# A selective-scan layer on one core: softplus in one function, three of sixteen products on GpSimd, the residual added by TensorE, row stores issued by SP

## The reference, cut to what matters

```
xi, z = split(xs @ W_in)                    # 64 channels each
xc = silu(causal_conv4(xi) + conv_b)
dt_r, B, C = split(xc @ W_x)                # 2, 16, 16
dt = softplus(dt_r @ W_dt + b_dt)           # 64 channels
h  = exp(dt * A) * h + dt * x * B           # per step, 64 channels x 16 states
y  = sum over states of h * C
out = x + ((y + xc * D_skip) * silu(z)) @ W_out
```

## Time and profile before

| | |
|---|---|
| median of three runs | 3129.49 us (3125.74 to 3132.32) |
| profiled execution, first to last instruction | 3123.6 us |
| around the span (median less span) | 5.9 us |
| triangle layers, first scan of the scan layer | to about 1254 us, at 1295.6 us |
| one chunk of the scan layer, steady | 56.7 us |
| busy: PE, DVE, ACT, POOL | 82%, 80%, 61%, 66% |

### The profile page before, as it was taken

The page is one execution under the profiler, slowest core; times in us unless marked ns, Lnnn a source line. Parts: engine busy times, 40 slices in busy tenths (PEclk is TensorE's granted clock), DMA queues, the critical chain, the costliest instruction groups (busy, mean ns, idle before and its releaser), DMA issues.

```text
span 3123.6 us, 40760 instructions
## 1 busy us (share of the span) xinstructions
PE 2573.1 (82%) x12954; PEld 756.1 (24%) x12954; DVE 2485.6 (80%) x2176; ACT 1914.4 (61%) x2402; POOL 2065.3 (66%) x1284
## 2 busy tenths in 40 slices
PE   5888878888788775688888888888888888888886
PEld 1233123331233211222222222222222222222221
DVE  5655656555555544599999999999999999999998
ACT  4534654346543343667777777677777776777772
POOL 2543245432444313298898888988988889889886
PEclk9999999999999988799999999999999999999999
DMA  4797327863279647667677677676775766767765
GB/s 162 241 325 212 102 67 255 294 205 102 72 241 313 192 133 181 132 146 181 147 165 167 144 177 163 148 181 148 162 170 145 179 160 148 180 148 162 171 145 117
DMA packets 257701, 537.53 MB, mean 172 GB/s; under 512 B 39608, under 2 KB 150656, under 8 KB 256688
## 3 DMA queue, kind: packets, MB, share of 16 engines
q1 hardware_dynamic: 215328, 444.01, 53.7%
q0 software_dynamic: 19040, 64.24, 7.7%
q10 hardware_dynamic: 23216, 27.74, 3.7%
HBM read 396.55 MB, written 139.33 MB: 172 GB/s over the span
## 4 chain that ended last, share of the span: by engine, by line
POOL 29%; issue 27%; PE 5%; DVE 2%; DMA 2%; ACT 1%; SPq 1%; POOLq 0%; ACTq 0%; DVEq 0%
POOL m_hs L500 18%; POOL m_sp_v L517 2%; POOL m_dtx L527 2%; POOL m_gated L506 2%; DMA t_tile<-band_out 1%; POOL m_dt L524 1%; POOL m_dt L520 1%; SPq L913 1%; DVE m_pb L472 1%; PE t_bank L1096 1%; PE t_bank L1057 1%; PE t_bank L1021 1%; POOL t_xc L1481 1%; DVE m_hs L477 1%; PE m_misc L230 0%
## 5 line engine op out<-in xcount | busy, mean ns | idle before, releaser
L500 POOL TENSOR_TENSOR m_hs<-m_hs,m_cs 128x1024 f32<-128x1024 f32 x512 | 1203.6, 2358 | 288.4 <-DVE m_hs L477 288.4
L477 DVE TENSOR_TENSOR_SCAN m_hs<-m_da,m_pb 128x1024 f32<-128x1024 f32 x512 | 1170.7, 2287 | 29.3 <-ACT m_da L399 4.2
L399 ACT ACTIVATE m_da<-m_dtb,m_a_neg 128x1020 f32<-128x1020 f32 x512 | 576.6, 1144 | 275.9 <-DMA m_dtb<-dt_rows 254.1
L282 PE MATMUL m_pb<-m_dtx,late 64*128 64x512 f32 x2048 | 583.5, 646 | 150.2 <-DVE m_hs L477 146.9
L265 PE MATMUL m_py<-m_hs,late 128*64 128x512 f32 x2048 | 565.8, 631 | 104.8 <-POOL m_hs L500 104.0
L472 DVE TENSOR_TENSOR m_pb<-m_pb,m_bs 128x1024 f32<-128x1024 f32 x512 | 619.7, 1210 | 20.9 <-PE m_pb L282 20.9
L1481 POOL TENSOR_TENSOR t_xc<-t_xc,big 128x512 f32<-128x512 f32 x96 | 120.1, 1271 | 338.8 <-DVE big L1387 338.8
L282 PEld LDWEIGHTS m_pb<-m_dtx,late 64*128 64x128 f32 x2048 | 163.4, 188 | 567.3 <-DVE m_hs L477 457.5
L1021 PE MATMUL t_bank<-late,t_lwin 128*128 128x256 f32 x816 | 217.3, 404 | 63.3 <-ACT big L1260 34.0
L1359 DVE SCALAR_TENSOR_TENSOR t_xc<-t_bank,t_vec,t_xc 128x512 f32<-128x512 f32 x96 | 72.0, 750 | 244.2 <-PE t_bank L1057 244.2
L1248 ACT ACTIVATE t_sq<-t_bank 128x512 f32<-128x512 f32 x192 | 105.5, 598 | 245.3 <-PE t_bank L1096 245.2
(11 more groups left out here) (166 smaller groups left out, 3591.3 us busy)
## 6 DMA issues: line engine op xcount, KB each, us to landing
m_dtb<-dt_rows SPq DMA_DIRECT2D x512, 512.0 KB, 6.1
late<-right_factor POOLq DMA_DIRECT2D x102, 512.0 KB, 5.5
right_factor<-t_tile SPq DMA_DIRECT2D x192, 256.0 KB, 3.5
t_tile<-band_out SPq DMA_DIRECT2D x183, 256.0 KB, 4.2
band_out<-t_vwin SPq DMA_DIRECT2D x48, 512.0 KB
band_out<-t_vwin SPq DMA_DIRECT2D x48, 480.0 KB
dt_rows<-m_dt ACTq DMA_DIRECT2D x64, 256.0 KB, 3.2
t_xc<-in_x_cm SPq DMA_DIRECT2D x4, 2048.0 KB, 14.6
```

Source lines behind the costliest of these rows:

```text
L282: m = nc.tensor.matmul(pb[s % 2][:, half(n)], spread[rows, dg, :], dtx[par][rows, half(q)], start=True, stop=True)
L399: nc.scalar.activation(da[:, s % DA_RING, :, 1:T], dtb[s % DTB_RING][:, :].rearrange("p (r t) -> p r t", t=T)[:, :, 1:T], ACT.Exp, scale=a ...
L477: nc.vector.tensor_tensor_scan(hs[:, s % H_RING, :], da[:, s % DA_RING, :, :].rearrange("p r t -> p (r t)"), pb[s % 2][:, :], 0.0, ALU.mul ...
L500: nc.gpsimd.tensor_tensor(hs[:, s % H_RING, :], hs[:, s % H_RING, :], cs[q][:, :], ALU.mult).then_inc(hc_ready, 1)
```

## The change

- dt: ScalarE applies Softplus straight from PSUM (two half tiles, table set "softplus" loaded before, the exp set after). The seven activations and GpSimd's six half tiles go; so do the buffers `sp_*`.
- Steps 5, 10 and 15 (`POOL_U`): TensorE writes the spread dt*x to `misc` instead of `pb`, ScalarE copies it to an SBUF tile `ub` (ring of two), GpSimd multiplies it by B there, and VectorE runs only the scan, with both inputs in SBUF.
- The residual: TensorE multiplies `xm` (moving operand, step 1 KB) by the identity `eye` into `py[1]`, on top of which the output product adds; ScalarE copies the sum to `fin`. VectorE's L484 goes.
- `dt_rows` and the stores of the result are issued by SP, shares 13 and 14, instead of ScalarE at share 14.
- `x` and `z` of the next chunk stand together in TensorE's share 5 and are taken together by one `silu`; the order of the uses of `misc` changes.
- The loop over chunks is written out in full.

```diff
+    POOL_U = (5, 10, 15)
+    UB_RING = 2
+        ub = [sb(f"ub{i}", [P, W]) for i in range(UB_RING)]
...
+        FIRST_USE = {op: i for i, op in enumerate(("x", "z", "dt", "bq0", "cq0"))}
+        USE = {op: i for i, op in enumerate(("u5", "bq1", "cq1", "u10", "x", "z", "dt", "bq0", "u15", "cq0"))}
...
         SHARES = {
-            "tensor": {0: [(PRE, "x")], 2: [(OWN, "bq1")], 4: [(OWN, "cq1")], 5: [(PRE, "dt")],
-                       8: [(PRE, "z"), (POST, "out")], 9: [(PRE, "bq0")], 11: [(PRE, "cq0")]},
-            "scalar": {1: [(PRE, "silu_x")], 3: [(OWN, "bq1")], 4: [(POST, "take1")], 5: [(OWN, "cq1")],
-                       6: [(PRE, "dt0"), (PRE, "dt1"), (PRE, "sp_abs")], 7: [(PRE, "sp_exp"), (PRE, "sp_ln"), (PRE, "sp_sum")],
-                       8: [(PRE, "sp_back"), (PRE, "sp_relu")], 9: [(PRE, "silu_z")], 10: [(PRE, "bq0")], 12: [(PRE, "cq0"), (OWN, "take0")],
-                       13: [(NEXT2, "xg0")], 14: [(POST, "store"), (PRE, "dt_rows")], 15: [(NEXT2, "xg1")]},
-            "vector": {9: [(POST, "out")]},
-            "gpsimd": {5: [(POST, "gate1")], 13: [(OWN, "gate0")], 7: [(PRE, "loss0"), (PRE, "log0")], 8: [(PRE, "dt0"), (PRE, "loss1")],
-                       9: [(PRE, "log1"), (PRE, "dt1")], 10: [(PRE, "dtx0")], 11: [(PRE, "dtx1")]},
-            "sync": {},
+            "tensor": {0: [(OWN, "u5")], 1: [(OWN, "bq1")], 3: [(OWN, "cq1")], 4: [(OWN, "u10")], 5: [(PRE, "x"), (PRE, "z")],
+                       7: [(PRE, "dt")], 8: [(POST, "out")], 9: [(PRE, "bq0")], 10: [(OWN, "u15")], 11: [(PRE, "cq0")]},
+            "scalar": {1: [(OWN, "u5")], 2: [(OWN, "bq1")], 4: [(POST, "take1"), (OWN, "cq1")], 5: [(OWN, "u10")], 6: [(PRE, "silu")],
+                       8: [(PRE, "dt")], 9: [(POST, "fin")], 10: [(PRE, "bq0")], 11: [(OWN, "u15")], 12: [(PRE, "cq0"), (OWN, "take0")],
+                       13: [(NEXT2, "xg0")], 15: [(NEXT2, "xg1")]},
+            "vector": {},
+            "gpsimd": {1: [(OWN, "u5")], 5: [(POST, "gate1")], 6: [(OWN, "u10")], 9: [(PRE, "dtx0")], 10: [(PRE, "dtx1")], 11: [(OWN, "u15")],
+                       13: [(OWN, "gate0")]},
+            "sync": {13: [(PRE, "dt_rows")], 14: [(POST, "store")]},
         }
...
-            with eng.Fori(1, CHUNKS - 4, 2) as k:
-                chunk(k, 1, (NEXT2, PRE, OWN, POST))
-                chunk(k + 1, 0, (NEXT2, PRE, OWN, POST))
-            chunk(CHUNKS - 3, 1, (NEXT2, PRE, OWN, POST))
+            for k in range(1, CHUNKS - 2):
+                chunk(k, k % 2, (NEXT2, PRE, OWN, POST))
...
+                    elif op[0] == "u":
+                        q, dg = divmod(int(op[1:]), DG)
+                        pe.wait_ge(dtx_ready, 2 * k + q + 1)
+                        for n in range(2):
+                            pe.wait_ge(misc_used[n], use(k, op))
+                        for n in range(2):
+                            rows = slice(D * n, D * n + D)
+                            nc.tensor.matmul(misc[n][:, :], spread[rows, dg, :], dtx[par][rows, half(q)],
+                                             start=True, stop=True).then_inc(misc_ready[n], 1)
...
+                    if s not in POOL_U:
...
+                    nc.tensor.matmul(py[1][:, :], eye[:, :], xm[:, :, SUB * k:SUB * k + SUB].rearrange("p t n -> p n t"),
+                                     start=True, stop=False, skip_group_check=True)
                     for q in range(2):
                         m = nc.tensor.matmul(py[1][D * q:D * q + D, :], w_out[:, :], gated[:, half(q)],
-                                             start=True, stop=True, skip_group_check=True)
+                                             start=False, stop=True, skip_group_check=True)
...
+                    elif op == "dt":
+                        a.preload_act_table_set("softplus")
                         if not early(k, 1):
                             a.wait_ge(dtx_ready, 2 * k)
                             a.wait_ge(dt_stored[1 - par], stores_of(k - 1, 1 - par))
+                        for q in range(2):
+                            a.wait_ge(misc_ready[q], use(k, "dt") + 1)
+                            nc.scalar.activation(dt[:, half(q)], misc[q][:, :], ACT.Softplus, bias=b_dt).then_inc(misc_used[q], 1)
+                        a.preload_act_table_set("natural_log_exp_and_others")
+                    elif op[0] == "u":
+                        j = pool_products(k, int(op[1:]))
+                        if j >= UB_RING:
+                            kk, i = divmod(j - UB_RING, len(POOL_U))
+                            a.wait_ge(h_ready, S * kk + POOL_U[i] + 1)
+                        for n in range(2):
+                            a.wait_ge(misc_ready[n], use(k, op) + 1)
+                            nc.scalar.copy(ub[j % UB_RING][:, half(n)], misc[n][:, :]).then_inc(misc_used[n], 1)
...
+                    a.wait_ge(o_ready, k + 1)
+                    if not early(k, 1):
+                        a.wait_ge(stored, 16 * G * k)
+                    nc.scalar.copy(fin[:, :], py[1][:, :]).then_inc(fin_done, 1)
...
+                    if s in POOL_U:
+                        j = pool_products(k, s)
+                        v.wait_ge(ub_ready, j + 1)
+                        products = ub[j % UB_RING][:, :]
...
+                    if op[0] == "u":
+                        j, q = pool_products(k, int(op[1:])), int(op[1:]) // DG
+                        for n in range(2):
+                            g_.wait_ge(misc_used[n], use(k, op) + 1)
+                        nc.gpsimd.tensor_tensor(ub[j % UB_RING][:, :], ub[j % UB_RING][:, :], bs[q][:, :], ALU.mult).then_inc(ub_ready, 1)
...
+                def pre(k, par, op):
+                    for q in range(2):
+                        sp.wait_ge(misc_used[q], use(k, "dt") + 1)
+                    if not early(k, 2):
+                        sp.wait_ge(da_ready, S * (k - 1))
+                    for n in range(2):
+                        sp.dma_start(dt_dram[par, :, :, n, :].rearrange("q d c -> d q c"),
+                                     dt[D * n:D * n + D, :].rearrange("d (q c) -> d q c", q=2)).then_inc(dt_stored[par], 16)
+                def post(k, par, op):
+                    sp.wait_ge(fin_done, k + 1)
+                    for g in range(G):
+                        sp.dma_start(out[:, SUB * k + g * NG:SUB * k + g * NG + SUB, :],
+                                     fin[DM * g:DM * g + DM, :].rearrange("p (n t) -> p n t", n=SUB)).then_inc(stored, 16)
```

More of the change, by code:

```diff
@@ L48, in mamba_layer @@
         gn_bias = sb("gn_bias", [P, 1])
-        (avg, w_in, conv_w, w_z, wx_dt, w_dt, w_bc, w_out, w_skip, vecs, a_log, spread, gather) = (t for t, _ in shared.weights)
+        (avg, w_in, conv_w, w_z, wx_dt, w_dt, w_bc, w_out, w_skip, vecs, a_log, spread, gather, eye) = (t for t, _ in shared.weights)
         w_conv = sb("w_conv", [P, TAPS // 2, P])
@@ L149, in use, with dve_products, pool_products @@
                 return FIRST_USE[name]
-            body = k if name in ("bq1", "cq1") else k - 1
-            if isinstance(k, int) and body == CHUNKS - 1:
-                return len(FIRST_USE) + len(USE) * body + ("bq1", "cq1").index(name)
+            body = k if name in OWN_USE else k - 1
+            if body == CHUNKS - 1:
+                return len(FIRST_USE) + len(USE) * body + OWN_USE.index(name)
             return len(FIRST_USE) + len(USE) * body + USE[name]
+        def dve_products(k, s):
+            return (S - len(POOL_U)) * k + s - sum(t < s for t in POOL_U)
+        def pool_products(k, s):
+            return len(POOL_U) * k + sum(t < s for t in POOL_U)
         def stores_of(k, par):
@@ L180, in schedule @@
-        def schedule(eng, name, pre, steps, post):
+        FIRST = {"vector": {9: [(PRE, "dtx0"), (PRE, "dtx1")]}, "gpsimd": {}}
+        def schedule(name, pre, steps, post):
             def share(k, par, kinds, s):
-                table = FIRST if kinds == (PRE,) and k == -1 and name in FIRST else FIRST_X if isinstance(k, int) and k == -2 and name in FIRST_X else SHARES
+                table = FIRST if kinds == (PRE,) and k == -1 and name in FIRST else FIRST_X if k == -2 and name in FIRST_X else SHARES
@@ L277, in steps @@
                         pe.wait_ge(dtx_ready, 2 * k + q + 1)
[L278 to L281, removed]
-                        m = nc.tensor.matmul(pb[s % 2][:, half(n)], spread[rows, dg, :], dtx[par][rows, half(q)],
-                                             start=True, stop=True)
-                    m.then_inc(b_ready, 1)
+                    if s not in POOL_U:
+                        if not (first and s < 2):
+                            pe.wait_ge(h_ready, g - 1)
+                        for n in range(2):
+                            rows = slice(D * n, D * n + D)
+                            m = nc.tensor.matmul(pb[s % 2][:, half(n)], spread[rows, dg, :], dtx[par][rows, half(q)],
+                                                 start=True, stop=True)
```

(17 more changed lines are left out.)

171 lines of the change are left out of this document (40 added, 131 removed).

## The result

The changed kernel takes 3162.07 us, the median of four runs (3153.21 to 3169.61), against 3129.97 us for the kernel before on the same chip (3125.74 to 3132.32). The ratio is 1.0094, with a 95% interval of 1.0069 to 1.0120: slower by 0.9%. The profiled span is 3160.9 us, 37.3 above the one before.

A forecast was written before the change was run, and what follows sets the result against it. VectorE bound the kernel before; after the change a cycle through VectorE, GpSimd and TensorE was to take 59.0 us a chunk against 56.7. 3129.5 + 69 for thirty cycles - 9 at the ends = 3189 us, range 3065 to 3240.

The forecast's parts named there:

- The lock: Scans from SBUF (steps 5, 10, 15) and GpSimd exclude each other, taken as 2.29 us of GpSimd's time each.
- Link 1: VectorE from product 6 to the end of scan 10, with product 9 waiting for TensorE's spread: 16.8 us.
- Link 2: GpSimd behind scan 10, never idle, through C products, two moved products, dtx, gate and scan 15's exclusion: 34.4 us.
- Link 3: TensorE from sum 2 through x and z to spread 6: 7.8 us, VectorE waiting some 3 us.
- The baseline and the ends: Chunk before 56.7 us, kernel before 3129.5 us; start shorter by about 4 us, last chunk and tail about -5.
- rival C: Exclusion holds and TensorE's identity product takes 3.6 us: 60.7 us a chunk, 3240 us in all; chance 0.10.
- The clock: TensorE may run at half clock after waiting about 3.7 us before sum 12; 1.4 us of slack takes most.
- Rival A: GpSimd and scans from SBUF do not shut each other out: 55.3 us a chunk, 3078 us in all; chance 0.24.
- Rival B: VectorE's own 51.5 us a chunk holds, as TensorE catches up everywhere: 2963 us in all; chance 0.06.
- Rival D: Exclusion lasts only half a scan's length: 56.9 us a chunk, 3128 us in all; chance 0.10.
- the ring: Chain per chunk through VectorE, GpSimd and TensorE back to VectorE's product 6: 59.0 us against 56.7 before.

## Why the prediction was right or wrong

It said slower, by a chunk of 59.0 us and 60 us in all. The sign, the mechanism and its place were right; the size was not: 57.94 us and 32 us by the medians, about half.

- **The lock** ("I take the whole"): there, as the forecast had it, and in both directions. It holds GpSimd for 1.9 to 2.0 us, by 4.26 and 3.26 us against 2.36 and 1.27; the C product beside scan 10 begins 0.16 us behind the scan, so nearly all of what is left of its 2.27 us is lost. The direction priced at "near 0.5" makes scan 15 1.9 us longer. The Trainium skill (SBUF — State Buffer, "Who interferes with whom") calls the port pair that the two engines share an exclusive lock, where the order of issue decides who blocks. That agrees with both directions here.
- **Link 1**, 16.8: measured 17.04 (product 6, one chunk earlier, at 2186.25, to scan 10's end at 2203.29). Product 9 waited 0.86 us, and the identity product took 1.89 where I took 1.9.
- **Link 2**, 34.4: measured 33.3 (2203.29 to the end of C product 2 at 2236.58), with no idle time on GpSimd, as forecast. This is the step that failed, and the term is mis-sized in its parts: I multiplied recorded lengths, 2.358, where instructions in a row follow each other at 2.31 to 2.33 (0.4 us over eleven of them) and half tiles at 1.22 to 1.24 instead of 1.27 (0.1); the lock took 2.0, not 2.29 (0.3); and C product 9, let go before scan 10 ended, had 2.1 us left at its end (0.25). Together 1.1 us a chunk, some 32 us in all, against a forecast growth of only 2.3 us a chunk: the term was 3% too large, and that halved the change. That the mistakes of the other links (0.24 too little, 0.27 too much) cancel is luck.
- **Link 3**, 7.8: measured 7.53 (2236.65 to 2244.18), with 3.11 us of VectorE's wait in it ("some 3").
- **The baseline and the ends**: the chunk before is 56.79 by the median and I used 56.7: 2.7 us in thirty. The start became shorter by 8.3 us, not 4; the tail longer by 4.2. From the first to the last scan I had 64 us and 32.0 came.
- **The identity product**: 1.9 was right. The reasons were loose: the step is 256 bytes, and the doubling seen on ScalarE happened to hold for TensorE. No row shows the "1.8 ns an element" behind rival C's 3.6 us; VectorE's 1039 ns for 512 elements are 2.0.
- **The clock**: a wait of 3.54 us before a sum (forecast "about 3.7 us"), and that sum at a granted clock of 0.5, 1.98 us instead of 1.08. The slack behind it took this, since the three links add up to the chunk without it.
- **Softplus, ScalarE, SP, the written-out loop**: no loss on the steady chunk, as said; the run with all of them, with z in another share and no other part, is 0.46 us a chunk faster, which the forecast did not have.
- **Rival A**, 55.3 without the lock and up to 0.5 more for the clock: measured 55.15 to 56.53, 55.75 on the mean, once the lock was taken out. **Rival B** (51.5) appears in no run; even the best order leaves 54.2. **Rival C** (3.6 us for the identity product) falls with its 1.89. **Rival D** supposed a lock of half a scan; it lasts 1.9 to 2.0 of 2.27 us.

## What to carry to other kernels

Before a product is moved to GpSimd so that VectorE's next instruction reads both inputs from SBUF, find the time of the lock on GpSimd's list: where it has slack (one product, 46.9 of 54.5 us) the move pays nearly in full, where it is a link of the ring (three products) it gives all of it back (1.9 us a chunk gained, 2.2 lost). Where one engine follows another through the same ring of tiles, price instructions in a row by the distance of their starts, not by their recorded length: 1% of a link of 34 us is a fifth of a gain of 2 us. Test a wait by taking away its nearest cause, and ask first whether the work that you move leaves the ring at all: z moved from one link to the next, and the chunk stayed.

## What the runs showed of the hardware that I had not expected

- A scan that reads both inputs from SBUF stopped GpSimd for 1.9 to 2.0 of its 2.27 us, though it works through an element in over two nanoseconds, and itself waited up to 2.2 us (4490 against 2287 ns). Where it found GpSimd idle it took 2265 ns, so SBUF itself is no slower for it than PSUM.
- TensorE's moving operand with a step of 256 bytes, 128x512 float32: 1.89 us for a product instead of 1.06.
- ScalarE's softplus of a 128x512 half from PSUM with a bias takes 683 ns, as long as a silu of that size with a bias (687, L341); the silu without one takes 595. The table load before it takes 1283 ns.

Their rows in the changed kernel, 2000 to 2940 us (table load, softplus, silu):

```profile
L351 ACT ACT_TABLE_LOAD x16 | 20.5, 1283 | 0.3
...
L357 ACT ACTIVATE m_dt<-m_misc,late 128x512 f32<-128x512 f32 x32 | 20.2, 683 | 0.2
L347 ACT ACTIVATE m_act<-m_misc 128x512 f32<-128x512 f32 x32 | 17.4, 595 | 75.3 <-POOL m_gated L466 75.3
```
